# Fused network: first slot of the later scans reordered, up products one place forward on three banks, gelus in groups of three

## The reference

```python
x = x + tanh(g_xattn[0]) * mixer(ctx, layernorm(x))     # state-space scan over 512 steps
x = x + tanh(g_ffn[0])   * bitlinear_network(layernorm(x))   # quantised 512 -> 2048 -> 512, gelu
x = x + tanh(g_xattn[1]) * attention(layernorm(x), ctx)
x = x + tanh(g_ffn[1])   * network(layernorm(x))         # 512 -> 2048 -> 512, gelu, biases
# mixer: for each of 16 state columns n:  state = state * exp(dt * A[:, n]) + (dt * u) * B[n];  y += state * C[n]
```

## Time and profile before

| | |
|---|---|
| device time, 3 runs | 972.73 to 973.33, median 973.03 us |
| the profiled execution, first to last instruction | 970.2 us; the median lies 2.8 us above it, which is the time outside the span |
| busy: PE, DVE, ACT, POOL | 819.7, 776.5, 661.0, 532.7 us |
| scans' halves, first of the three later passes | DVE 248.16 to 375.3 us |
| table loads on ACT for decays and for the gelus of the scans | 27 and 24, 1283 ns each |

### The profile page before, as it was taken

How to read it: one execution, slowest core, us unless ns; L and a number is a source line. 1 busy time by engine, 2 the same in 40 slices (tenths; PEclk the granted TensorE clock), 3 DMA queues, 4 the chain that set the end, 5 groups by cost and what they waited for, 6 DMA issues and landing times. The chain is left out here.

```text
span 970.2 us, 9341 instructions
## 1 busy us (share of the span) xinstructions
PE 819.7 (84%) x2770; PEld 406.0 (42%) x2810; DVE 776.5 (80%) x905; ACT 661.0 (68%) x984; POOL 532.7 (55%) x461
## 2 busy tenths in 40 slices
PE   6721247799799999999799999998899999898999
PEld 2210023354344344454344444444343444446887
DVE  4589997895989998985889998976899998964333
ACT  4699979673699963773599873772799863714442
POOL 0698786302899884212999882214998881012000
PEclk9755558799899999998899999999899999999999
DMA  8179982001299965301399963301599961201231
GB/s 299 20 136 218 272 197 46 1 1 44 44 202 235 237 139 141 109 2 43 61 218 239 234 137 109 109 1 44 114 221 209 236 143 53 109 1 44 87 109 66
DMA packets 46819, 119.57 MB, mean 123 GB/s; under 512 B 5793, under 2 KB 6945, under 8 KB 46257
## 3 DMA queue, kind: packets, MB, share of 16 engines
q0 software_dynamic: 16128, 58.73, 32.3%
q1 hardware_dynamic: 30640, 60.24, 18.4%
HBM read 56.03 MB, written 4.19 MB: 62 GB/s over the span
## 5 line engine op out<-in xcount | busy, mean ns | idle before, releaser
L1669 POOL TENSOR_TENSOR work<-du,bcast 128x1024 f32<-128x1024 f32 x128 | 352.3, 2780 | 32.5 <-ACT bcast L868 31.8
L1272 DVE TENSOR_TENSOR_SCAN pair<-pair,work 128x512 f32<-128x512 f32 x256 | 299.3, 1215 | 33.6 <-ACT pair L883 29.9
L883 ACT ACTIVATE pair<-dt,a_neg 128x512 f32<-128x512 f32 x256 | 165.7, 681 | 20.2 <-DVE work L1279 17.2
L654 PE MATMUL bank<-stage,ring 128*128 128x512 f32 x384 | 172.9, 593 | 5.7 <-ACT bcast L868 4.4
L1279 DVE TENSOR_TENSOR work<-pair,ccast 128x1024 f32<-128x1024 f32 x128 | 156.7, 1225 | 11.6
L1684 POOL DMA_DIRECT2D u<-work x112 | 122.0, 1089 | 35.7 <-DVE work L1279 15.8
L439 PE MATMUL bank<-xd,pick 128*128 128x512 bf16 x108 | 48.2, 446 | 82.4 <-ACT bcast L868 56.0
L654 PEld LDWEIGHTS bank<-stage,ring 128*128 128x128 f32 x384 | 71.8, 190 | 80.5 <-issue 70.9
L1655 POOL TENSOR_SCALAR fst<-fst 128x1 f32<-128x1 f32 x32 | 9.3, 290 | 169.9 <-DVE fst L1506 169.6
L668 PE MATMUL bank<-ring,stage 128*128 128x512 f32 x192 | 85.6, 594 | 1.7 <-ACT hx L1152 1.7
L439 PEld LDWEIGHTS bank<-xd,pick 128*128 128x128 bf16 x128 | 13.0, 102 | 140.1 <-ACT bcast L868 89.7
(11 more groups left out here) (169 smaller groups left out, 1501.5 us busy)
## 6 DMA issues: line engine op xcount, KB each, us to landing
u<-work POOLq DMA_DIRECT2D x112, 512.0 KB, 5.9
ring<-ffn_dram SPq DMA_DIRECT2D x120, 256.0 KB, 4.7
ring<-ffn_dram SPq DMA_DIRECT2D x16, 512.0 KB, 3.4
xres<-x_dram SPq DMA_DIRECT2D x4, 1024.0 KB, 5.4
stage<-w_dram SPq DMA_DIRECT2D x1, 4096.0 KB, 17.0
stage<-w_dram SPq DMA_DIRECT2D x4, 1024.0 KB, 7.5
out_dram<-stage SPq DMA_DIRECT2D x16, 256.0 KB, 2.1
ctxT<-ctxT_dram SPq DMA_DIRECT2D x4, 512.0 KB, 6.2
```

Of the source, the lines that this page charges most:

```text
L654: last = pe.matmul(banks[2 + f % 2][:], piece(b, f)[:, k * P:(k + 1) * P], xnT[:, k, :], start=k == 0, stop=k == J - 1)
L883: act.activation(pairs[s % DECAYBUFS][:, q, :], dt[:, p * HALF + q, :], ACT.Exp, scale=a_neg[:, p * HALF + q, n:n + 1]).then_inc(s_decay, 1)
L1272: dve.tensor_tensor_scan(pair[:, q, :], pair[:, q, :], rows[:, q, :], 0.0, ALU.mult, ALU.add).then_inc(s_scan, 1)
L1669: pool.tensor_tensor(work[:, s % SCANBUFS, :, :], du[:, p * HALF:(p + 1) * HALF, :], bcast[:, n % 2, :].unsqueeze(1).broadcast_to([P, HALF ...
```

## The change

Four things, all in the three passes with `rest=True`.

1. Slot 4. PE makes the second key product ahead of the second broadcast. ACT copies each projection as soon as it is there, and makes the decays of half 2 after all these copies instead of at the slot's start.
2. Up products stand one place earlier, (4, 3) to (8, 2), and use banks 1, 2 and 3 by turns, so f waits for the gelu of f - 3.
3. Gelus stand in groups of three at (5, 1), (6, 0), (6, 3), (7, 2) and (8, 1), and the last alone at (8, 3): 6 groups instead of 8, and 12 table loads of a pass instead of 16.
4. Down pairs start at (8, 3) and fill (9, 3) and (11, 1); `fourth` stands after half 25 instead of 27. The first energies wait for all gelus, since they use bank 1.

```diff
-FFN_UP = {(5 + f // 4, f % 4): f for f in range(FT)}
-FFN_DOWN = {(9, 0): (0, 0), (9, 1): (0, 2), (9, 2): (0, 4), ...
-FOURTH_SLOTS = {(11, 0): 0}
+FFN_UP = {(4 + (f + 3) // 4, (f + 3) % 4): f for f in range(FT)}
+FFN_DOWN = {(8, 3): (0, 0), (9, 0): (0, 2), (9, 1): (0, 4), ...
+FFN_GELUS = {(5, 1): (0, 1, 2), (6, 0): (3, 4, 5), (6, 3): (6, 7, 8), (7, 2): (9, 10, 11), (8, 1): (12, 13, 14), (8, 3): (15,)}
+UP_BANKS = (1, 2, 3)
+FOURTH_SLOT = 10
...
             def f_up(b, f):
-                if f >= 2:
-                    pe.wait_ge(s_fgelu, b * FT + f - 1)
-                else:
+                if f >= 3:
+                    pe.wait_ge(s_fgelu, b * FT + f - 2)
+                elif f == 0:
                     pe.wait_ge(s_xnTc, b * 2 * T + 2 * T)
+                    pe.wait_ge(s_qk, (b + 1) * 2 + 2)
...
+            def first_slot(b, m):
+
+                decays(m, b, 4, 0, 0)
+                norm_copy(b, 5)
+                qk_copy(m, b, 0)
+                copy_next(m, 4, 0, 0)
+                qk_copy(m, b, 1)
+                copy_next(m, 4, 0, 1)
+                decays(m, b, 4, 0, 1)
+                norm_copy(b, 6)
+                norm_copy(b, 7)
```

More of the change, by code:

```diff
@@ L500, in energies @@
                     pe.wait_ge(s_qk, b * 2 + 2)
+                    if b:
+                        pe.wait_ge(s_fgelu, (b - 1) * FT + FT)
                 pe.matmul(banks[1][:], qk[:, 0, j * P:(j + 1) * P], qk[:, 1, :],
@@ L647, in f_up @@
             def f_up(b, f):
-                if f >= 2:
-                    pe.wait_ge(s_fgelu, b * FT + f - 1)
-                else:
+                if f >= 3:
+                    pe.wait_ge(s_fgelu, b * FT + f - 2)
+                elif f == 0:
                     pe.wait_ge(s_xnTc, b * 2 * T + 2 * T)
+                    pe.wait_ge(s_qk, (b + 1) * 2 + 2)
                 pe.wait_ge(*loaded(b, f))
                 for k in range(J):
-                    last = pe.matmul(banks[2 + f % 2][:], piece(b, f)[:, k * P:(k + 1) * P], xnT[:, k, :],
+                    last = pe.matmul(banks[UP_BANKS[f % 3]][:], piece(b, f)[:, k * P:(k + 1) * P], xnT[:, k, :],
                                      start=k == 0, stop=k == J - 1)
@@ L662, in f_down @@
                     else:
-                        pe.wait_ge(s_fgelu, b * FT + FT)
+                        pe.wait_ge(s_fgelu, b * FT + FT - 1)
+                elif r == 0 and f == FT - 1:
+                    pe.wait_ge(s_fgelu, b * FT + FT)
                 k = down_load(r, f)
@@ L815, in pass_ @@
                         weights(slot)
+                    if slot == QK_SLOT and rest:
+                        qk_products(m, prev, 1)
                     bcast_next(m, slot, 0, 1)
@@ L822, in pass_ @@
                             norm_transpose(b, 7)
+                        else:
+                            qk_products(m, prev, 1)
                     if rest:
@@ L1151, in f_gelu @@
                 act.wait_ge(s_fmm1, b * FT + f + 1)
-                act.activation(h_tile(f), banks[2 + f % 2][:], ACT.Gelu, bias=b1[:, f:f + 1]).then_inc(s_fgelu, 1)
+                act.activation(h_tile(f), banks[UP_BANKS[f % 3]][:], ACT.Gelu, bias=b1[:, f:f + 1]).then_inc(s_fgelu, 1)
             def f_gelus(b, slot, place):
-                for i in (place, place + 1):
-                    if (slot, i) in FFN_UP:
-                        f_gelu(b, FFN_UP[slot, i])
+                for f in FFN_GELUS.get((slot, place), ()):
+                    f_gelu(b, f)
             def pass_(b, rest=True):
@@ L1164, in pass_ @@
                     opening(m)
-                for slot in range(4, SLOTS):
+                if rest:
+                    first_slot(b, m)
+                for slot in range(5 if rest else 4, SLOTS):
                     decays(m, prev, slot, 0, 0)
@@ L1168, in pass_ @@
                         decays(m, prev, slot, 0, 1)
-                        if rest:
-                            norm_copy(b, 5)
                     copy_next(m, slot, 0, 0)
@@ L1175, in pass_ @@
                         qk_copy(m, prev, 0)
-                    if not rest:
+                    if rest:
+                        f_gelus(b, slot, 0)
+                    else:
                         weights(slot)
@@ L1184, in pass_ @@
                         qk_copy(m, prev, 1)
-                        if rest:
-                            norm_copy(b, 6)
-                            norm_copy(b, 7)
                     if rest:
-                        f_gelus(b, slot, 0)
+                        f_gelus(b, slot, 1)
                     decays(m, prev, slot, 1, 0)
@@ L1193, in pass_ @@
                     attention(m, prev, slot, 1, 0)
+                    if rest:
+                        f_gelus(b, slot, 2)
                     decays(m, prev, slot, 1, 1)
@@ L1198, in pass_ @@
                     if rest:
-                        f_gelus(b, slot, 2)
+                        f_gelus(b, slot, 3)
                     if slot == ZS_SLOT:
@@ L1597, in pass_ @@
                     half(m, prev, slot, 0, 1)
-                    if rest and (slot, 0) in FOURTH_SLOTS:
-                        fourth(b, FOURTH_SLOTS[slot, 0])
                     half(m, prev, slot, 1, 0)
                     half(m, prev, slot, 1, 1)
+                    if rest and slot == FOURTH_SLOT:
+                        fourth(b, 0)
                 if rest:
```

4 lines of the change are left out of this document (2 added, 2 removed).

## The result

The changed kernel takes 967.2 us (median, 964.05 to 970.02) against 973.33 for the kernel before (972.73 to 976.74): a ratio of 0.993, 95% interval 0.9909 to 0.995. It is faster by 6.1 us. The forecast was 959.1, a gain of 13.9; the stated range ended at 967.5. The profiled execution spans 961.9 us against 970.2.

The account below looks back on a forecast made before the run. It took a gelu loop in which ACT and PE wait for each other, and PE's lateness at the turn, as the bounds. 3 x 4.64 = 13.9 us off 970.2 gives 956.3, plus 2.8 outside the span 959.1; range 953 to 967.5.

Parts of the forecast that it names:

- The first up product: Slot 4: PE starts it at 255.3 instead of 260.86 us, 5.6 us earlier.
- half 3's wait: DVE's half 3 no longer waits for its decays and starts at 260.17 instead of 261.49 us.
- The loop and the groups: Gelu loop of ACT and PE: 11.4 us for three halves, old loop 11.6; half 19 starts at 321.75 instead of 325.15.
- POOL: POOL gives half 7's input at 276.1, DVE asks at 276.2; 0.6 us of lateness would be hidden at half 8.
- The clock in slot 4: Rival: PE's clock falls to half rate at the first ups, costing 2.2 us a pass, total 965.7 us; chance 0.17.
- The third maximum, `fourth`, the down pairs: After half 25 DVE newly waits 0.8 us for energies, PE idles some 2 us for `fourth`; downs start at 315.9.
- The turn: PE arrives first, transposes start with DVE's gating, DVE's update comes at 378.1 instead of 382.74, waiting about 0.7 us.
- Nothing in the closing changes: Work after the last pass's turn, like the first pass, was to stay unchanged.
- the looser loop: Rival: third gelu finds its product ready, three places take 10.95 us, 1.8 us more per pass, 953.8 us; chance 0.12.
- the three faster cases: Chances of a faster kernel: the forecast with smaller errors 0.56, the clock 0.17, the looser loop 0.12; stated together as 0.86.

Follow-up runs that it names:

- the threes by themselves: Changed kernel with the old order of slot 4, keeping early up products, three banks, groups of three and moved downs: 979.67 us, 1.0058 to the kernel before.
- late biases: Changed kernel with POOL's four output-bias additions moved from slots 4 and 5 to slots 7 and 8: 960.65 us, 0.9863 to the kernel before.
- a second profile of the same kernel: The changed kernel measured and profiled again with no edit: 965.93 us, 0.9924 to the kernel before.
- all four edits: Changed kernel with slot-4 idle products, POOL's biases moved later, ACT's broadcast copy ahead of table load and decays, twelve idle products at the turn: 955.9 us, 0.9831.
- two repairs: Changed kernel with seven idle PE products in slot 4 and POOL's bias additions moved to slots 7 and 8: 958.05 us, 0.9837 to the kernel before.
- idle products alone: Changed kernel with seven PE products nobody reads added in slot 4 of later passes: 964.69 us, 0.9897 to the kernel before.
- the reordering by itself: Kernel before with only the new order of slot 4; ups, paired gelus and downs as before: 962.43 us, 0.9887.

## Why the prediction missed

**The first up product: right.** Forecast 255.3, measured 255.02, and half 3's wait went.

**The loop and the groups: right.** Forecast 11.4 us, measured 11.38 in four groups. What my text did not see is how little this is worth: the threes by themselves lose, and even with the repairs they come with 0.1 to 0.8 us a pass.

**POOL: the step that failed.** I wrote that POOL gives the input of half 7 at 276.1, DVE asks at 276.2, and that a lateness would be hidden by the wait at half 8. So I put this wait at nothing, and I asked the wrong consumer. POOL's reading of `bcast` also holds ACT's next copy into it, at (6, 0), which by my own times was due at about 274, and behind that copy stand the three gelus. It was not hidden by the wait at half 8; it was that wait. The measured price is 131.11 - 129.80 = 1.3 us in a pass whose clock holds, and late biases with a clock that holds bring half 8 from 33.48 to 32.16. Rows 7 held the start and duration that showed it, 272.57 + 3.55 = 276.1.

**The clock in slot 4: named as the first rival, at 2.2 us a pass and 0.17.** In the profile it happened in two passes of three, and cost 1.7 us at half 5. In a second profile of the same kernel it happened in none. PE worked 1.31 and 0.98 of 2 us in the windows from 252 and 254. In the second profile the same stretch (windows from 250.75 and 252.75, its pass starting 1.25 us earlier) held 1.31 and 0.96 us, and the clock stayed at 1.00. So neither the order nor that much thin work settles whether it falls, and the 0.17 cannot be judged from these passes: it fell in four of the fifteen with this order. Nor did I see that my 5.6 us between 260.86 and 255.3 held 2.3 of clock alone: the row that I read for the old start was itself at half rate. The Trainium skill, TensorE: Matmul & The Clock Gate, What's actually happening, says, of the clock's rise at the start of a kernel, that the number of products before the switch differs from run to run of one kernel. The three passes and the two profiles agree with it as far as the same instructions met another clock; of the start of a kernel they say nothing.

**The third maximum, `fourth`, the down pairs: right.** 0.69 us for 0.8, PE's wait for `fourth` 1.88 for some 2. `fourth` itself came at 350.83 for 349.4, by as much later as half 5 was.

**The turn: the order right, the wait mis-sized.** PE came first and DVE's wait fell, as forecast. But I stopped at "the transposes start with DVE's gating" and did not read what 3.5 us without work do to PE: the clock was at 0.50 to 0.58 at the turn in all three passes, where the kernel before had no fall, since PE was late there. The wait was 1.21 in passes 1 and 3, and 0.75 in pass 2, where the fall came only behind the transposes, against 0.7 forecast.

**"Nothing in the closing changes": wrong by 1.87 us.** PE's granted clock is 0.50 from 870 to 872 and 0.70 from 872 to 874 in the profile. The kernel before passed the same thin place (0.66 and 0.79 us of work in the windows from 876 and 878) at 1.00 throughout. No edit touches that place, and the profiles sort by their falls: 160.2 us from the last update to the end with none (the kernel before alone), 161.4 to 161.7 with a short fall in the closing, 162.8 to 162.9 with one twice as long, 162.1 to 162.4 with a fall at the last turn. So the 1.87 us are the clock's, about 1.4 in the closing and the rest at the last turn. The part in the closing needs no edit: the kernel before with idle products in slot 4, which is the kernel before from there on, took 161.7.

In the sum: of 13.9 us the three passes missed 2.0 + 1.1 + 2.5 = 5.5, and the two walls explain nearly all: with both away the three passes give 4.3, 4.9 and 4.4 us instead of 4.64. That the time is then 958.05, where the forecast is 959.1, is in part luck: that kernel is 16.4 us below the kernel before of its own group (974.41), some 3 more than its passes give, and its profiled execution, the slowest of its five, is 9.8 below. The tail took 1.9, and the gaps gave 1.7. This 1.7 is luck too: in either gap the fall behind the turn was one step shorter than in the kernel before, 1.65 us each (last section), and the falls at the turn took back 0.4 and 1.2. And that 967.2 lies inside the range, 0.3 us from its end, is luck: the range was made for the clock (965.7), and the wait for POOL, which it held at nothing, filled it as well. What is left between 8.3 us of span and 6.1 of medians is the spread of the executions: 964.05 to 970.02, of which the profiled one is the fastest. (Two small slips of the working change nothing: the looser loop gives 953.7 and not 953.8, and the chances of the three faster cases add up to 0.85 and not 0.86.)

A version better than both kernels came from this: all four edits, 955.9 us, 0.9831. Its interval (to 0.9853) lies wholly below both that were measured for the changed kernel (from 0.9909 and from 0.9897); against two repairs alone (0.9837) it is not told apart.

## What to carry to other kernels

When a step moves earlier, ask of every buffer it touches who reads the old content last, not only who needs the new. The end of that read is a start time for everything behind the writer. Repair two near walls together before judging either: idle products alone moved the update of a pass by -0.5 to 0.9 us, late biases alone by 0.05 where the clock fell, both together by 1.3 to 2.2. Before reordering for an engine that pauses, try what its clock alone gives: 22 idle products in an existing pause made the kernel before 9.7 us faster by its median, the reordering by itself 10.3. And an engine brought early to a meeting point stands idle there, which can cost its clock: PE stood idle 3.55 us and was granted 0.57 behind it.

## What the hardware showed unexpectedly

- PE's granted clock also falls where PE is nearly always busy. Windows of PE, kernel before, behind the first and the second turn:

```profile
436.00:438.00 2.00, 2.00 (x5) 0.85 0.00 0
438.00:440.00 2.00, 1.67 (x4) 0.50 0.00 0
440.00:442.00 2.00, 2.00 (x6) 0.50 0.00 0
652.00:654.00 2.00, 1.67 (x4) 0.61 0.00 0
```

  The first fall is twice as long as the second. In the windows from 426 to 436 PE had worked all of every 2 us; what stands just ahead of the first fall are products with 16 rows (L486, 16x512). Where the turn itself had no fall, the gap between update and next scan was 80.05 to 80.07 us with the long one, 78.36 to 78.42 with the short one, and 76.72 to 76.73 in the two gaps without any: about 1.65 us a step. Which one came varied between kernels that are the same there, so a comparison of two single profiles can be off by several us for this alone.
- POOL's instructions have no fixed price: the input of a half, the same form each time, took 2.94, 3.22, 3.53 and 3.85 us for four halves in a row in the second pass of the changed kernel. An estimate from POOL's row needs the worst of its neighbours.
- The clock stood at 1.00 each time idle products filled a pause of PE: in 21 passes in slot 4, in nine at the turn, where without them it fell in 16 of 21 passes with threes. They are not free where PE can come late: in four of those nine turns they held the transposes up by 0.5 us.
